# Low parts of h of units 4 to 6 subtracted on VectorE instead of GpSimd, and both y tiles normalized in one run, in a one-layer attention and MLP kernel

## The reference

```python
q1, q2, k, v = (split_heads(x @ W, 16) for W in (Wq1, Wq2, Wk, Wv))   # head size 16
scores = einsum('bhqd,bhkd->bhqk', concat([q1, q2]), repeat(k, 2)) / sqrt(16)
p = softmax(where(causal, scores, min))
y = einsum('bhqk,bhkd->bhqd', p, repeat(v, 2))
y = y[:, :16] - sigmoid(x @ Wlam) * y[:, 16:]
x = layernorm(x + merge_heads(y) @ Wo)
h = (g * sigmoid(g)) * u,   g = x @ gate.T,   u = x @ up.T     # 1024 shared + 128 routed columns
x = layernorm(x + h_shared @ down_s.T + comb_w * (h_routed @ down_r.T))
```

## Time and profile before

| | |
|---|---|
| time, median of 3 runs | 462.35 us (460.74 to 462.37) |
| profiled execution: time, span | 462.41 us, 460.7 us |
| PE busy | 422.0 us (92%) |
| DVE busy | 278.3 us (60%) |
| ACT busy | 237.3 us (52%) |
| POOL busy | 249.2 us (54%) |

### The profile page before, as it was taken

The page is one execution under the profiler, slowest core; times in us unless marked ns, Lnnn a source line. Parts: engine busy times, 40 slices in busy tenths (PEclk is TensorE's granted clock), DMA queues, the critical chain, the costliest instruction groups (busy, mean ns, idle before and its releaser), DMA issues.

```text
span 460.7 us, 10485 instructions
## 1 busy us (share of the span) xinstructions
PE 422.0 (92%) x4074; PEld 343.9 (75%) x4074; DVE 278.3 (60%) x679; ACT 237.3 (52%) x536; POOL 249.2 (54%) x335
## 2 busy tenths in 40 slices
PE   4693978899999999999999999999999999997995
PEld 4571447795898669985898679985898579855995
DVE  3256346753758466755857476855767488747464
ACT  4454833467254943577264943486355921493240
POOL 8273636457254944667355935576365921493152
PEclk9796797799999999999999999999999999999998
DMA  7492590354023710372024511380024410000000
GB/s 265 122 267 73 178 257 12 117 140 92 1 69 111 159 47 21 107 179 56 23 81 121 135 47 31 99 208 27 23 85 115 116 47 1 4 1 23 1 25 23
DMA packets 34753, 40.41 MB, mean 88 GB/s; under 512 B 4240, under 2 KB 28304, under 8 KB 34448
## 3 DMA queue, kind: packets, MB, share of 16 engines
q1 hardware_dynamic: 34704, 39.75, 31.8%
HBM read 27.94 MB, written 11.53 MB: 86 GB/s over the span
## 4 chain that ended last, share of the span: by engine, by line
PE 70%; POOL 9%; DVE 8%; ACT 4%; DMA 3%; SPq 3%; issue 2%; POOLq 0%; DVEq 0%; ACTq 0%
PE ff L727 11%; PE ff L728 10%; PE ff L729 10%; PE ring L791 7%; POOL prob L447 6%; PE ybank L873 4%; PE ybank L727 3%; PE ring L786 3%; PE ybank L728 3%; PE ybank L729 3%; PE ring L845 3%; DVE neg_max L1121 2%; PE ff L817 2%; PE ring L727 2%; ACT prob L566 1%
## 5 line engine op out<-in xcount | busy, mean ns | idle before, releaser
L437 POOL TENSOR_TENSOR h_lo<-h_full,h_hi 128x256 fp32r<-128x256 f32 x72 | 53.1, 738 | 100.6 <-ACT h_hi L515 100.6
L1113 DVE TENSOR_REDUCE neg_max<-ring 128x2 f32<-128x384 f32 (+3 forms) x154 | 90.1, 637 | 28.1 <-PE ring L791 27.4
L447 POOL TENSOR_SCALAR_AFFINE_SELECT prob<-prob 128x512 f32<-128x512 f32 x128 | 83.1, 681 | 17.1 <-ACT prob L566 16.2
L727 PE MATMUL ff<-x1T_hi,wg_lo 128*128 128x256 f32 x288 | 87.0, 302 | 0.0
L566 ACT ACTIVATE prob<-ring 128x512 f32<-128x512 f32 x144 | 78.3, 619 | 5.2 <-PE ring L845 5.2
L728 PE MATMUL ff<-x1T_lo,wg_hi 128*128 128x256 f32 x288 | 80.9, 281 | 0.0
L729 PE MATMUL ff<-x1T_hi,wg_hi 128*128 128x256 f32 x288 | 80.8, 281 | 0.0
L1149 DVE COPY yv<-ybank 128x256 f32<-128x256 f32 x64 | 27.0, 422 | 53.1 <-PE ybank L873 52.7
L873 PE MATMUL ybank<-prob,v_ones 128*32 128x256 f32 (+1 forms) x1024 | 56.5, 336 | 2.0 <-POOL prob L447 1.8
L727 PEld LDWEIGHTS ff<-x1T_hi,wg_lo 128*128 128x128 f32 x288 | 54.7, 190 | 3.1 <-issue 1.3
L574 ACT ACTIVATE gate_t<-ff 128x256 f32<-128x256 f32 x72 | 27.7, 385 | 56.0 <-PE ff L729 56.0
(11 more groups left out here) (187 smaller groups left out, 977.1 us busy)
## 6 DMA issues: line engine op xcount, KB each, us to landing
q_stack<-qk_parts_dram SPq DMA_DIRECT2D x48, 256.0 KB, 4.5
qk_parts_dram<-parts SPq DMA_DIRECT2D x72, 128.0 KB
k_stack<-qk_parts_dram SPq DMA_DIRECT2D x48, 128.0 KB, 4.3
xt_raw<-xT SPq DMA_DIRECT2D x8, 256.0 KB, 2.9
xz<-x SPq DMA_DIRECT2D x8, 256.0 KB, 2.9
out<-xz SPq DMA_DIRECT2D x7, 256.0 KB, 2.2
prob<-w_gu SPq DMA_DIRECT2D x1, 1152.0 KB, 6.3
yv<-w_gu SPq DMA_DIRECT2D x1, 1024.0 KB, 7.4
```

The source lines that it names most:

```text
L437: pool.tensor_tensor(h_lo[:, n, :], h_full[:, n % RING, :], h_hi[:, n, :].bitcast(F32), ALU.subtract).then_inc(h_lo_done, 1)
L447: pool.affine_select(out=v, in_=v, compare_op=ALU.is_ge, fill=0.0, base=0, pattern=[[0, 2], [HALF, 2], [0, 2], [1, HALF]], channel_multipl ...
L727: pe.matmul(o, lhs_lo, rhs_hi, start=first, stop=False)
L1113: dve.tensor_reduce(neg_max[:, columns.start:columns.stop, i], ring[u % RING][:, 0:len(columns) * keys].rearrange("p (h k) -> p h k", k=keys),
```

## The change

DVE gets a new function, `h_second`, which makes the low part of h of units 4, 5 and 6 in iterations 1 to 7, one ahead of each of the first three copies of the group loop. POOL no longer does these three; before units 7 and 8, which stay with POOL, it waits until DVE's three are done. In DVE's list, `normalize_y` of tile 1 now follows that of tile 0 directly, and the multiplications of units 7 and 8 come behind both. In ACT's list `yT_first` moves ahead of the copy of unit 7's high part.

```diff
@@ gpsimd, iteration
-                    if has_prev and g - 1 in FF_SCORES:
-                        n = FF_SCORES[g - 1]
-                        h_rests(i - 1, range(n, n + 1))
                 if has_prev:
+                    pool.wait_ge(h_lo_done, (i - 1) * FF_UNITS + FF_Y0)
                     h_rests(i - 1, range(FF_Y0, FF_UNITS))
@@ scalar, iteration
                     gate_tanh(i - 1, FF_Y0)
                     gate_tanh(i - 1, FF_Y1)
+                yT_first(i)
+                if has_prev:
                     h_first(i - 1, FF_Y0)
-                yT_first(i)
-                if has_prev:
                     h_first(i - 1, FF_Y1)
@@ vector
+            def h_second(b, n):
+                dve.wait_ge(h_hi_done, b * FF_UNITS + n + 1)
+                dve.wait_ge(h_lo_done, b * FF_UNITS + n)
+                dve.tensor_tensor(h_lo[:, n, :], h_full[:, n % RING, :], h_hi[:, n, :].bitcast(F32), ALU.subtract).then_inc(h_lo_done, 1)
@@ vector, iteration
                     if has_prev and g + 1 in FF_SCORES:
                         mlp_unit(i - 1, FF_SCORES[g + 1])
+                    if has_prev and g in FF_SCORES:
+                        h_second(i - 1, FF_SCORES[g])
                     evacuate_pv(i, g)
...
                 normalize_y(i, 0, *attn)
+                normalize_y(i, 1, *attn)
                 if has_prev:
                     mlp_unit(i - 1, FF_Y0)
-                normalize_y(i, 1, *attn)
-                if has_prev:
                     mlp_unit(i - 1, FF_Y1)
                 yT_second(i)
```

More of the change, by code:

```diff
@@ L680, in iteration @@
                     gate_tanh(i - 1, FF_Y1)
-                    h_first(i - 1, FF_Y0)
                 yT_first(i)
                 if has_prev:
+                    h_first(i - 1, FF_Y0)
                     h_first(i - 1, FF_Y1)
```

## The result

The changed kernel takes 458.31 us (median of 8 runs, 457.38 to 460.24), the kernel before 461.38 us (8 runs, 460.74 to 462.58). The ratio is 0.9934 with a 95% interval of 0.9911 to 0.9957: 0.66% faster, where 0.6% was forecast. The profiled execution has a span of 457.2 us against 460.7.

The account below looks back on a forecast made before the run. PE, busy 92% of the span, was taken as the bound. POOL's 1.4 us plus y's 1.35 gave 2.75 off the profiled 462.41, 459.7, less 0.06 for the median: 459.6 us, range 458.0 to 462.4.

Parts of the forecast that it names:

- The gap at the back-transposes: PE's wait for DVE's subtraction of y tile 1, claimed to shrink from 0.60 to 0.12 us.
- the gap named for it: End of the transposed scores: PE's value products of group 7 start 0.29 us late, released by POOL.
- POOL's term: POOL's last selection of group 7 ends 0.27 us earlier per iteration, until ACT limits; 1.4 us in all after hold-ups.
- The hold-up of POOL: A DVE subtraction delays POOL by up to 0.43 us, costing 0.05 per iteration; one taken in half of six iterations.
- DVE's cover: Subtractions ahead of DVE's copies of groups 1 and 2 fit margins of 1.46 and 1.97 us; cost 0.
- The y term: PE starts the output projection 0.20 us earlier per iteration, not 0.48, because yT_lo is late; 1.35 us in all.
- Iteration 7: The last iteration: 0.15 us put down for POOL's part and 0.15 for the y part.
- B: Rival: only one of the two terms arrives, time 461.0 us; chance 0.27.
- C: Rival: more than priced, PE keeps the whole 0.48 us per iteration at y, time 458.0 us; chance 0.05.
- A: Case that both terms arrive as priced, time 458.5 to 460.4 us; chance 0.52.
- D: Rival: nothing measurable, each saving taken up by an engine read as having slack, 462.3 us; chance 0.07.
- E: Rival: POOL's back-to-back selections starve DVE, group 2's copy comes late, 463.7 or some 472 us; chance 0.09.

Follow-up runs that it names:

- e1: Changed kernel with the old order around y on DVE and ACT, so only the low parts of h move to DVE; ratio 0.9970 to the kernel before.
- e2: Changed kernel without h_second, POOL making all low parts of h, so only the new order around y remains; ratio 0.9975 to the kernel before.
- e3: Kernel before with only unit 6's low part of h moved to DVE, order around y as before; ratio 0.9951 to the kernel before.
- e6: Changed kernel with DVE's second-norm statistics moved behind the multiplications of unit 6; ratio 0.9929 to the kernel before.
- e5: Changed kernel with yT_lo on DVE between the multiplications of units 7 and 8, not behind both; ratio 0.9902 to the kernel before.
- e8: Changed kernel with DVE's three subtractions ahead of the copies of groups 3, 4 and 5 instead of 0, 1 and 2; ratio 0.9923 to the kernel before.

## Why the prediction was right

*The number.* The forecast was 459.6 us and the time is 458.31. Of these 1.3 us, 0.97 are the kernel before, which the forecast took at 462.35 and which measured 461.38 over its eight runs; the saving is 3.07 us where 2.75 was forecast.

*The limits.* Each part of the change shortened the stretch that it was meant to: e1 and e2 show it. The gap at the back-transposes was read rightly. At the end of the transposed scores POOL's last selection was the right thing to read, but the gap named for it, 0.29 us before group 7, is 0.32 after; the 0.25 us came out of the products of groups 5 and 6.

*POOL's term* was 0.27 us per iteration and measured 0.23 (17.26 to 17.03). The saving of units 4 and 5 is worth nothing, as said (e3 has the whole gain). That ACT becomes the limit is seen in POOL's pause before group 7 and shown by e6: without ACT's wait of 0.29 the stretch falls by a further 0.18. The hold-up of POOL that I had put at up to 0.43 us in half the iterations is 0.25, in every iteration, since the lists meet at the same point each time; ACT's limit hides nearly all of it, until e6 takes that limit away.

*DVE's cover.* The margins held: PE's value products of groups 3 and 4 are not released by a copy in any of the traces, so the cost of 0 stands. The subtraction takes 0.42 us for unit 5 and 0.55 for unit 6, against 0.43 from L1174.

*The y term* was 0.20 and measured 0.17 (8.33 to 8.16). Its mechanism is as described: 1.24 us from the second reciprocal to the subtraction (I had taken 1.2), then 1.91 to yT_lo (1.92). That yT_lo takes back 0.28 of the gain is shown by e5.

*Iteration 7* gave more than the 0.30 put down: from its scores to the projection 24.99 before, 24.62 after, 0.37.

*A term that I did not have.* The stretch from the projection to the next scores went from 25.68 to 25.61. In the other kernels it is 25.64 to 25.69, so it is tied to no edit. In places PE issues its 256-column products closer together: from 248.05 to 249.18 in the trace after, ten of them start 0.113 us apart, where at the same place before, from 249.72 to 250.90, it is 0.118. Why was not tried and stays open.

*The sum.* From iteration 1's transposed scores to the end the two traces take 363.0 and 360.0 us. Of these 3.0 us the first stretch gave 1.45 over the seven iterations, where 1.4 was forecast, and the second 1.11, where 1.35 was. The other 0.42 lie in the third stretch (0.28) and behind the last projection (0.14), and belong to neither term. That the total comes so near to 2.75 is in that part luck.

*The rivals.* B, that only one term arrives, would have needed 461.0 or a period of 51.0; e1 and e2 look like that, the whole change does not. C, that PE keeps the whole 0.48 us at y, would have needed a second stretch of 7.85 instead of 8.16, although 458.31 lies nearer to its 458.0 than to A's middle. D, that nothing is measurable, is out by the interval of the ratio. E was settled by e8.

## What to carry to other kernels

Count what an offload saves from the point where the relieved engine last stopped to wait: savings ahead of that point only make its wait longer, and here two of three moved subtractions brought nothing and one of them harm. When an early result frees a consumer, look for the next operand that it needs: the work put off to make the first one early may stand ahead of the second. And when one limit of three engines with nearly equal loads is removed, the next stands a few tenths of a microsecond behind it, so small defects that were hidden begin to count.

## What the runs showed of the hardware

The subtraction on DVE, with two SBUF inputs, and the selection on POOL, which reads SBUF, hold each other up when they meet, and the lost time appears in the duration of the one that came second: 0.83 instead of 0.42 us for the subtraction behind a selection, 0.92 instead of 0.67 for a selection that started 0.02 us behind a subtraction. In both directions the hold-up is shorter than what was left of the other's recorded duration (0.25 of 0.40 us, and 0.41 of 0.56), so by these records the second did not wait for the first to end. This is the row of POOL's timeline after:

```profile
258.46 0.92 POOL L447 TENSOR_SCALAR_AFFINE_SELECT prob<-prob 128x512 f32<-128x512 f32 x1
```

Single runs of one kernel spread by 1.5 to 5.5 us although the periods repeat to 0.1 us. Between the traces, one of each kernel, a difference of that size lies at the start, where no edit has touched anything yet: iteration 1's transposed scores begin at 94.5 us in e2_y_only, where the granted TensorE clock over the first 95 us is 0.87, at 96.2 in e1_h_only (0.84), and at 97.7 in the kernel before (0.82). That the clock is the whole cause was not tested, nor that it is the cause of the spread among runs of one kernel. It is why the periods, and not single times, carry the argument above.
